# Attention blocks of a cross-attention and mixture-of-experts kernel: events moved between the 18 slots of a block

## What is computed

```python
x = x + xattn(ctx_1024, layernorm(x), ...)
x = x + ffn(layernorm(x), ...)

# xattn: latents are the 1024 rows, x is the context
q = lat @ Wq
kv = concatenate([x, lat], axis=1) @ Wkv
k, v = split(kv, 2, axis=-1)
dots = einsum('bhid,bhjd->bhij', q, k) * scale
attn = softmax(dots, axis=-1)
out = einsum('bhij,bhjd->bhid', attn, v)
return merge_heads(out) @ Wout

# ffn: shared expert and the 4 best of 32 experts, in 4 of 8 groups, with a capacity of 320 rows each
shared = silu(xf @ sg) * (xf @ su) @ sd
```

## Time and profile before

| | us |
|---|---|
| median of 3 runs | 1649.9 |
| lowest, highest | 1648.56, 1650.05 |
| the profiled execution, its own time | 1647.04 |
| its span in the profile | 1645.3 |
| PE busy in the span | 1513.9 |
| DVE busy | 1050.6 |
| POOL busy | 940.0 |
| ACT busy | 796.0 |

### The profile page before, as it was taken

The page is one execution under the profiler, slowest core; times in us unless marked ns, Lnnn a source line. Parts: engine busy times, 40 slices in busy tenths (PEclk is TensorE's granted clock), DMA queues, the critical chain, the costliest instruction groups (busy, mean ns, idle before and its releaser), DMA issues.

```text
span 1645.3 us, 23810 instructions
## 1 busy us (share of the span) xinstructions
PE 1513.9 (92%) x8086; PEld 1067.2 (65%) x8086; DVE 1050.6 (64%) x1574; ACT 796.0 (48%) x1501; POOL 940.0 (57%) x751
## 2 busy tenths in 40 slices
PE   3899999999999999999999999988899999999995
PEld 2565555555655555565565555546779999999995
DVE  7556666576565665767767776556656566666662
ACT  3355444544444445544454344533336566666662
POOL 4457766666566765766667777784343343334333
PEclk8899999999999999999999999998899999999998
DMA  3032440000000000000011000101246666667664
GB/s 99 16 80 70 101 91 11 24 15 10 18 8 22 15 10 24 15 11 15 10 28 31 27 28 27 44 30 58 81 161 167 175 191 180 172 177 193 171 173 89
DMA packets 99282, 117.93 MB, mean 72 GB/s; under 512 B 10595, under 2 KB 78181, under 8 KB 99173
## 3 DMA queue, kind: packets, MB, share of 16 engines
q1 hardware_dynamic: 82149, 96.97, 20.1%
q0 software_dynamic: 17056, 19.97, 6.2%
HBM read 74.93 MB, written 35.06 MB: 67 GB/s over the span
## 4 chain that ended last, share of the span: by engine, by line
PE 72%; DVE 15%; ACT 6%; POOL 3%; issue 2%; DMA 1%; ACTq 0%; SPq 0%; DVEq 0%; POOLq 0%
PE ps_o L947 13%; PE ps_t L804 8%; PE ps_m L909 8%; PE ps_m L804 8%; PE ps_st L804 7%; PE ps_st L932 6%; DVE arena_r L1307 5%; PE ps_st L936 5%; ACT arena L1590 3%; PE ps_m L841 3%; PE ps_o L841 3%; PE ps_t L967 2%; DVE arena L1318 2%; PE ps_t L1014 2%; PE ps_t L954 2%
## 5 line engine op out<-in xcount | busy, mean ns | idle before, releaser
L744 POOL TENSOR_TENSOR arena<-arena 128x512 f32<-128x512 f32 (+1 forms) x512 | 660.3, 1292 | 345.9 <-ACT arena L1590 307.3
L1590 ACT ACTIVATE arena<-ps_st 128x512 f32<-128x512 f32 (+1 forms) x576 | 327.3, 596 | 463.2 <-PE ps_st L936 430.3
L1307 DVE TENSOR_REDUCE arena_r<-ps_m 128x1 fp32r<-128x1107 f32 x256 | 334.2, 1306 | 179.4 <-PE ps_m L909 175.4
L779 POOL DMA_INDIRECT acc_rows<-arena,ids x96 | 150.8, 1571 | 267.1 <-ACT arena L1653 239.5
L932 PE MATMUL ps_st<-arena_r 128*128 128x512 f32 (+1 forms) x576 | 247.9, 430 | 27.9 <-ACT arena L1590 27.8
L947 PE MATMUL ps_o<-arena 128*64 128x512 f32 (+1 forms) x1152 | 268.5, 601 | 0.0
L936 PE MATMUL ps_st<-arena_r 68*128 68x512 f32 (+2 forms) x576 | 229.7, 399 | 1.9 <-DVE arena_r L1314 1.9
L909 PE MATMUL ps_m<-arena_r 128*128 128x370 f32 x768 | 194.7, 362 | 31.0 <-DVE arena_r L1307 23.1
L909 PEld LDWEIGHTS ps_m<-arena_r 128*128 128x128 f32 x768 | 130.1, 192 | 118.3 <-DVE arena_r L1307 65.6
L932 PEld LDWEIGHTS ps_st<-arena_r 128*128 128x128 f32 (+1 forms) x576 | 106.9, 186 | 106.7 <-ACT arena L1590 84.2
L947 PEld LDWEIGHTS ps_o<-arena 128*64 128x64 f32 (+1 forms) x1152 | 74.2, 137 | 143.2 <-issue 132.0
(11 more groups left out here) (211 smaller groups left out, 1870.9 us busy)
## 6 DMA issues: line engine op xcount, KB each, us to landing
arena<-in_L_ffn_wg_dram SPq DMA_DIRECT2D x32, 512.0 KB, 4.6
arena<-in_L_ffn_wu_dram SPq DMA_DIRECT2D x32, 512.0 KB, 6.4
arena<-in_L_ffn_wd_dram SPq DMA_DIRECT2D x32, 512.0 KB, 3.9
x_slots<-route SPq DMA_DIRECT2D x5, 2176.0 KB, 12.9
arena<-x_slots SPq DMA_DIRECT2D x32, 272.0 KB, 2.7
arena_r<-arena_r SPq DMA_DIRECT2D x30, 275.2 KB, 3.7
arena<-in_L_xattn_Wkv_dram SPq DMA_DIRECT2D x32, 128.0 KB, 2.4
arena<-x_slots SPq DMA_DIRECT2D x32, 68.0 KB, 2.4
```

Source lines behind the costliest of these rows:

```text
L744: pool.tensor_tensor(total, probsT[0:rows, h, 0, :] if kt == 1 else total, probsT[0:rows, h, kt, :], ALU.add).then_inc(added, 1)
L779: pool.indirect_dma_start(out=dst[:, :], in_=y_sb[par][:, c, 0:w], in_offset=None, compute_op=ALU.add, out_offset=bass.IndirectOffsetOnAxi ...
L1307: dve.tensor_reduce(neg[h][:, c:c + 1], ps_m[:, :, 0:PIECE_W], AX.XY, ALU.max, negate=True)\
L1590: act.activation(probsT[0:rows, h, kt, :], ps_st[0:rows, n % 2, :], ACT.Exp).then_inc(exp_done, 1)
```

## The change

Within each block, events move to other slots; nothing is computed differently and the same instructions are issued.
- `sum` moves from (0, 8), in front of slot (1, 0), to behind slot (1, 0).
- The second output product of a block moves from (1, 6) of the next block to (0, 2) of the one after (`out_b`).
- `own_max[1]` moves from (0, 0) to (0, 1). In heavy blocks `own_max[2]` goes to (0, 3) and `own_max[3]` ahead of the value products at (0, 5); key piece 1 goes from (0, 3) to (0, 4), the query from ahead of the value products at (0, 5) to (0, 6), behind them.
- In light blocks `last_values` go from (0, 5) to (0, 4), the query's second copies and split from (0, 5) to (0, 3), `more_values` and the next `row` from (1, 6) to (1, 7).
- Of the extra events, `b` and `ring_early` go to other slots.

```diff
--- before.py
+++ after.py
@@ -80,27 +80,35 @@
         last_values = values(old, prev, (6, 7, 8))
         own_max = [own("max", d, 1, i) for i in range(4)]
         next_max = [nxt("max", n, 0, i) for i in range(4)]
-        out = [old("out", prev, i) for i in range(2)]
-        after = {(0, 8): [own("row", d, 1), old("sum", prev)],
+        out_a = old("out", prev, 0)
+        out_b = ("out", (d - 2) % QUADS, 1), int(d < 2)
+        after = {(0, 1): [own_max[1]],
+                 (0, 8): [own("row", d, 1)],
+                 (1, 0): [old("sum", prev)],
                  (1, 1): [],
                  (1, 2): [old("norm", prev), next_max[0]],
-                 (1, 3): first_values + [next_max[1]]}
+                 (1, 3): first_values + [next_max[1]],
+                 (1, 4): [out_a, next_max[2]]}
         if project:
-            after[0, 0] = [own_max[0]] + project_k(0) + [own_max[1], k_low[0]]
-            after[0, 2] = project_k(2) + [own_max[2], k_low[2]]
-            after[0, 3] = project_k(1) + [k_low[1]]
-            after[0, 5] = project_q() + [q_again] + last_values + [q_low, own_max[3]]
-            after[1, 4] = [out[0], next_max[2]]
+            after[0, 0] = [own_max[0]] + project_k(0)
+            after[0, 1] += [k_low[0]]
+            after[0, 2] = project_k(2) + [out_b]
+            after[0, 3] = [own_max[2], k_low[2]]
+            after[0, 4] = project_k(1)
+            after[0, 5] = [own_max[3], k_low[1]] + last_values
+            after[0, 6] = project_q() + [q_again, q_low]
             after[1, 5] = [nxt("v", pp, 0), next_max[3]]
-            after[1, 6] = more_values + [nxt("row", n, 0), out[1]]
+            after[1, 6] = more_values + [nxt("row", n, 0)]
             after[1, 7] = [nxt("v", pp, 1)]
             after[1, 8] = [nxt("v", pp, 2)]
         else:
-            after[0, 0] = [own_max[0]] + project_q() + [own_max[1]]
-            after[0, 3] = [own_max[2]]
-            after[0, 5] = [q_again] + last_values + [q_low, own_max[3]]
-            after[1, 4] = [out[0], next_max[2]]
-            after[1, 6] = [out[1], next_max[3]] + more_values + [nxt("row", n, 0)]
+            after[0, 0] = [own_max[0]] + project_q()
+            after[0, 2] = [out_b]
+            after[0, 3] = [q_again, q_low, own_max[2]]
+            after[0, 4] = last_values
+            after[0, 5] = [own_max[3]]
+            after[1, 6] = [next_max[3]]
+            after[1, 7] = more_values + [nxt("row", n, 0)]
         if d == 0:
             after[1, 1] = [own("w", 1)] + after[1, 1]
         if d == 2:
@@ -123,7 +131,7 @@
         put(block, 1, 3, "mid", *events)
 
     def b(block, *events):
-        put(block, 1, 6, "row", *events)
+        put(block, 1, 7 - block % 2, "row", *events)
 
     def c(block, *events):
         put(block, 0, 5, "end", *events)
@@ -135,7 +143,7 @@
         put(block, 1, 0, "end", *events)
 
     def ring_early(block, *events):
-        put(block, 0, 2, "end", *events)
+        put(block, 0, 3, "end", *events)
 
     for j in range(FILLS):
         put(1 + j, 0, 6, "end", ("fill", j))
@@ -224,15 +232,14 @@
             for n, (ev, back) in enumerate(slot):
                 place = "row" if ev[0] == "row" else "mid" if n == len(slot) - 1 else None
                 plan += [(new, T) for at, new in more if at == place]
-                late = (ev, T - back) == (("out", LAST_D - 1, 1), LAST_T)
-                if 0 <= T - back < TURNS and not late:
+                if 0 <= T - back < TURNS:
                     plan.append((ev, T - back))
                     if (ev, T - back) == (("out", LAST_D - 1, 0), LAST_T):
                         plan.append((("out", LAST_D - 1, 1), LAST_T))
-                elif T == 0 and ev[0] == "out":
+                elif T == 0 and ev[0] == "out" and ev[1] == LAST_D:
                     plan.append((("cen", ev[2]), 0))
             plan += [(new, T) for at, new in more if at == "end"]
-    end = [ev for slot in slots for ev, back in slot if back == 1]
+    end = [ev for slot in slots for ev, back in slot if back == 1 and ev != ("out", LAST_D - 1, 1)]
     assert [ev[0] for ev in end] == ["av"] * 3 + ["sum", "norm", "out", "out"]
     scats = [[("scat", g, i) for i in range(SCATTERS)] for g in range(GROUPS)]
```

## The result

The changed kernel takes 1809.06 us, median of 4 runs (1804.09 to 1812.71), against 1649.97 us before. The ratio is 1.0964, interval 1.0944 to 1.0984. The forecast was 1753 us with a range up to 1790: the direction was right, the size was not. It came out 159 us slower where 103 were forecast.

The account below looks back on a forecast made before the run. The prediction took PE's issued work plus PE's waits as the bound: 1647.0 us profiled + 72 (heavy blocks) + 16 (light blocks) + 18 (clock) = 1753 us, range 1695 to 1790.

Parts of the forecast that it names:

- Heavy block, both walks: Heavy block: first-half waits +2.8 us, query waits +2.5, filled empty pair -0.5; +4.8 us, 15 times, +72 us.
- Light block: Light block: gains from filled slots 1.7 us, losses 2.65; net +1.0 us, 16 times, +16 us.
- (a): Light block: the sum no longer covers DVE's mask product ahead of the next half score product, +0.75 us.
- (b): Light block: the sum and its reciprocal come later, so the maximum behind the value products waits, +0.7 us.
- (c): Light block: the next block's fourth maximum loses the output product ahead of it, +0.6 us.
- (d): Light block: the query's second copies and split precede the third maximum's reduce, delaying the fourth maximum, +0.4 us.
- (e): Light block: the next block's row is now one slot from its user, +0.2 us.
- The clock: Heavy block: one fall to the 1.2 GHz level in each, 1.2 us, 15 times, +18 us.
- Rival 1: Attention blocks: same waits but the clock holds at full level, 1735 us; chance 0.2.
- Rival 2: Heavy blocks: two slow-clock stretches in each and the upper wait sizes, 1787 us; chance 0.12.
- Rival 3: Exp loop: filling empty pairs wins if banks and copies come free before PE asks, 1612 us; chance 0.07.
- The exp loop: Score products alternating between two banks, each freed by its exp: a pair of empty slots costs 0.5 us, a single one nothing.

Follow-up runs that it names:

- experiment 4: Changed kernel with every wait kept, but zero-weight matmuls feeding PE in the heavy blocks' first-half and query waits: 1757.4 us (ratio 1.0654).
- Experiment 6: Changed kernel with only the two first-half waits of heavy blocks filled with zero-weight matmuls (9 and 6): 1787.0 us (ratio 1.0821).
- experiment 10: Kernel before the change with only the next block's first maximum moved from (1, 2) to (1, 1): 1648.7 us (ratio 0.9997).
- experiment 8: Changed kernel with heavy-block query and output product moves undone, sum back at (0, 8), light-block query split behind third maximum, last values at (0, 5): 1631.9 us.

## Why the prediction was wrong in size

- **Heavy block, both walks: right in mechanism, somewhat small.** Places and order of the waits are in the trace, and their ends to 0.2 us. With the waits filled a heavy block takes 5.9 us more on average (experiment 4) where the sum had 4.8: 89 us instead of 72, within its bounds of 3.5 and 6. What makes up the rest was not tested; the walk named restarts that it left out.
- **Light block: right.** In the block at 204 us the waits of (a) to (d) are there: (a) 1.16 us behind the row instead of 1.25, (b) 1.10 instead of 0.7, (c) 0.47 instead of 0.6, (d) 0.39 instead of 0.4; (e) was not tested. At full clock the net is 0.95 us a block where 1.0 was forecast, 15 us instead of 16. Since the gains and (e) were not measured one by one, the net may owe something to luck.
- **The clock: the step that failed.** "I expect one fall in each: 15 x 1.2 = +18 us." It cost 52 us by experiment 4, and some 4 us more in light blocks (24 slow us against 13 before, at 0.4). The price of a slow us was about right, 1.2 us for 3.5 (0.34) against 0.4 measured. The number of slow us was not: 130 in the heavy blocks in place of 15 x 3.5 = 53. The one fall behind each query came, 15 of 15. Two things were missing: 10 more falls in the first half of the block, and the length, 5.2 us a fall on average where the prediction took the 3.5 of the earlier trace rows. It charged nothing for waits of 2.2 and 1.6 us, although the wait ahead of that very fall was 1.06 us. Experiment 6 shows that filling these shorter ones, two in a block, gives back 22 us alone. The upper bound, "1.7 twice", named the falls at the first-half waits, and its 51 us is close to what was measured, but partly by luck: there were fewer falls than two a block, each was longer, and each slow us cost 0.4 and not 0.5.
- **The row of one fall was read too narrowly.** The earlier trace rows is called the one fall inside the attention part. The clock of the kernel before was at the lower level in its first light block too:

```profile
52.00:60.00 8.00, 7.78 (x26) 6.28 (x26) 3.18 (x3) 3.56 (x7) 1.65 (x2) 0.69 0.00 0
66.00:72.00 6.00, 5.41 (x18) 3.23 (x20) 3.74 (x5) 2.80 (x5) 5.57 (x5) 0.72 0.00 1
```

- **The sum with what was measured:** heavy 89, light 15, clock 56: 160 us, where the result is 159. With 18 us for the clock the measured waits would have given about 1770 us, inside the range; it was the clock that carried the result out of it. Rival 1 (clock holds) gave 1735; the kernel with the clock held in the heavy blocks takes 1757. Rival 2 (more falls), given 0.12, was the true case. Its 1787 is 22 us short: some 11 us in the clock (45 against 56), 9 in the heavy waits (80 against 89), and 3 because it started from the profiled execution. Rival 3 asked that banks and copies be free before PE asks; they were not.
- **The rule that the prediction cited.** The Trainium skill (TensorE: Matmul & The Clock Gate, section "HAM oscillation — how this bites in real kernels") describes a kernel that pays for its return to full clock at every tile, since each waits (there for DMA). This case agrees for the query's wait, with a fall in 15 of 15 heavy blocks, and in part for the first half's, with a fall in 10 of 15. The prediction took one fall a block from it, and the kernel has more than one wait a block.
- **The exp loop: half right.** The changed kernel did break empty pairs, but by experiment 10 breaking one alone brings 0.5 us in 6 of 15 heavy blocks and nothing measurable in the total.

## What to carry to other kernels

Where a planned order has PE wait at two or three places of a block, price the waits once for their length and once for the clock: here some 104 us of longer blocks came with 56 us more for the slow clock. Count every wait, not only the longest. In a pool of two banks a job waits for the reader of the job two before it, so before one is put in between, look at the order in which that reader works (here DVE's: reduce, then split). Give a chain of copy and split a long product as cover. A step that seems to stand in no one's way on an engine that is not the busiest (the weight split, 0.7 us) can still be the difference between a hidden step and a wait.

## What was unexpected of the hardware

- Filling waits with matmuls that compute nothing made a kernel faster: 405 extra matmuls, 1809.1 to 1757.4 us. Zero weights were enough to hold the granted clock at 1.00 in the heavy block shown.
- The clock fell behind waits of 1.95 us (the output product at 315.36 took 2.07 us, in the heavy block before 1.13 after the same wait). The same wait is not followed by a fall each time: it stands in all 15 heavy blocks, and the clock fell at it in 10. Why not in the other five was not tested.
- One and the same DVE operation, the weight split of 128x512, took from 0.61 to 2.84 us in experiment 8.
